# A non-local block on one core: the small tiles are allocated first and the large ones start on multiples of 2 KB

## What is computed

```
q = theta_w @ x + theta_b          # 256 x 1024 positions
p = maxpool2(x)                    # 1024 channels x 256 positions
k = phi_w @ p + phi_b              # 256 x 256
v = g_w @ p + g_b                  # 256 x 256
a = softmax(q.T @ k * 256**-0.5)   # 1024 x 256
out = z_w @ (v @ a.T) + z_b + x    # 1024 x 1024
```

## The kernel before

| kind | function | stationary | moving | columns | matmuls in all |
|---|---|---|---|---|---|
| q | `project_q` | theta | x_split | 512 | 3072 |
| k | `project_k` | phi | xp | 256 | 1536 |
| v | `project_v` | xp | g | 256 | 1536 |
| s | `scores` | q | k | 256 | 1536 |
| a | `attend` | vt | pt | 512 | 768 |
| z | `project_out` | z | att | 256 | 5376 |

## Time and profile before

### The profile page before, as it was taken

The page is one execution under the profiler, slowest core; times in us unless marked ns, Lnnn a source line. Parts: engine busy times, 40 slices in busy tenths (PEclk is TensorE's granted clock), DMA queues, the critical chain, the costliest instruction groups (busy, mean ns, idle before and its releaser), DMA issues.

```text
span 2162.6 us, 40114 instructions
## 1 busy us (share of the span) xinstructions
PE 2082.1 (96%) x13824; PEld 1898.1 (88%) x13824; DVE 1566.2 (72%) x2617; ACT 1293.1 (60%) x2228; POOL 1377.9 (64%) x835
## 2 busy tenths in 40 slices
PE   6799999999999999999999999999999999999996
PEld 5699989998998899899989988998999899999996
DVE  6877767876777777678767777776787677787765
ACT  4565656665656655566646656565666566666553
POOL 4666667765667666667656676665676566776653
PEclk9899999999999999999999999999999999999998
DMA  6455566564666565575655664655656556656535
GB/s 224 132 200 187 178 203 213 175 207 158 200 218 198 173 201 174 192 233 176 196 163 189 214 216 156 202 179 185 233 175 196 167 185 214 221 177 203 186 102 175
DMA packets 213070, 409.54 MB, mean 189 GB/s; under 512 B 12688, under 2 KB 15760, under 8 KB 212880
## 3 DMA queue, kind: packets, MB, share of 16 engines
q1 hardware_dynamic: 212736, 406.90, 56.9%
q10 hardware_dynamic: 144, 0.01, 0.0%
HBM read 272.64 MB, written 134.22 MB: 188 GB/s over the span
## 4 chain that ended last, share of the span: by engine, by line
PE 94%; DVE 2%; issue 2%; DMA 1%; ACT 0%; POOL 0%; SPq 0%; DVEq 0%
PE bank L748 94%; DMA x<-x 1%; DVE pt_raw L597 1%; DVE z_lo L636 0%; DVE phi_lo L561 0%; DVE x_top L615 0%; DVE x_bot L615 0%; DVE pooled L569 0%; ACT probs L408 0%; DVE att_f L627 0%; POOL x_split_lo L494 0%; POOL pt_lo L504 0%; POOL att_f L507 0%; DVE q_lo L575 0%; POOL att_lo L512 0%
## 5 line engine op out<-in xcount | busy, mean ns | idle before, releaser
L494 POOL TENSOR_TENSOR x_split_lo<-x,x_split_hi 128x1024 fp32r<-128x1024 f32 x256 | 617.4, 2417 | 278.4 <-ACT x_split_hi L320 278.4
L748 PE MATMUL bank<-att_hi,z_hi 128*128 128x256 f32 x1792 | 497.4, 278 | 8.1 <-POOL att_lo L512 5.1
L748 PE MATMUL bank<-att_lo,z_hi 128*128 128x256 f32 x1792 | 496.7, 277 | 0.0
L748 PE MATMUL bank<-att_hi,z_lo 128*128 128x256 f32 x1792 | 496.6, 277 | 0.0
L597 DVE STREAM_TRANSPOSE pt_raw<-probs 32x256 f32<-32x256 f32 x1024 | 446.1, 436 | 17.5 <-ACT probs L408 0.9
L512 POOL TENSOR_TENSOR att_lo<-att_f,att_hi 128x512 fp32r<-128x512 f32 (+1 forms) x192 | 282.9, 1480 | 216.7 <-ACT att_hi L359 216.7
L748 PE MATMUL bank<-x_split_hi,theta_hi 128*128 128x512 f32 x1024 | 407.7, 398 | 12.2 <-POOL x_split_lo L494 10.0
L748 PE MATMUL bank<-x_split_lo,theta_hi 128*128 128x512 f32 x1024 | 404.6, 395 | 0.0
L748 PE MATMUL bank<-x_split_hi,theta_lo 128*128 128x512 f32 x1024 | 404.0, 395 | 0.0
L615 DVE TENSOR_TENSOR x_top<-bank,x_top 128x512 f32<-128x512 f32 x512 | 334.9, 688 | 86.6 <-PE bank L748 79.7
L320 ACT ACTIVATE x_split_hi<-x 128x1024 fp32r<-128x1024 f32 x256 | 270.8, 1058 | 162.3 <-PE bank L748 158.8
(11 more groups left out here) (64 smaller groups left out, 4139.0 us busy)
## 6 DMA issues: line engine op xcount, KB each, us to landing
x<-x SPq DMA_DIRECT2D x256, 512.0 KB, 4.0
x_top<-x SPq DMA_DIRECT2D x128, 512.0 KB, 7.0
x_bot<-x SPq DMA_DIRECT2D x128, 512.0 KB, 7.8
out<-x_top SPq DMA_DIRECT2D x128, 512.0 KB, 3.6
out<-x_bot SPq DMA_DIRECT2D x128, 512.0 KB, 4.7
x_top<-theta_wt SPq DMA_DIRECT2D x4, 256.0 KB, 6.1
x_bot<-phi_wt SPq DMA_DIRECT2D x4, 256.0 KB, 9.5
x_top<-g_wt SPq DMA_DIRECT2D x4, 256.0 KB, 8.7
```

Source lines behind the costliest of these rows:

```text
L494: nc.gpsimd.tensor_tensor(flat(lo), flat(x_chunk(s, c)), raw(flat(hi)), ALU.subtract).then_inc(x_ready, 1)
L748: last = nc.tensor.matmul(dst, stationary(a), moving(b), start=start and n == 0, stop=stop and n == len(PRODUCTS) - 1, skip_group_check=re ...
```

## The change

The small tiles (`bias`, `phi_bias`, `negmax`, `rowsum`, `rowinv`: 32 or 64 bytes each after rounding, 192 bytes together) are allocated ahead of the large ones, followed by an unused tile `line_pad` of 704 bytes. 1152 + 192 + 704 = 2048, so `theta_hi` starts at byte 2048, and as all tiles up to `pt_lo` have sizes that are multiples of 2048 bytes, each starts on such a multiple. `att_f` loses its eighth block and moves behind `att`: `att_hi` starts at 206848 (101 x 2048), `att_lo` 7168 bytes behind it, on a multiple of 1024, and `att_f` at 221184 (108 x 2048). The fourth sum of the z weights goes to the first block of `probs` instead, and for that VectorE waits once for the transposes of the first step, which read `probs`. No instruction is added, taken away or moved otherwise; no shape changes.

```
+        bias = sb("bias", [P, NB], f32)
+        phi_bias = sb("phi_bias", [P, DT], f32)
+        negmax = sb("negmax", [P, NT], f32)
+        rowsum = sb("rowsum", [P, NT], f32)
+        rowinv = sb("rowinv", [P, NT], f32)
+        sb("line_pad", [P, 176], f32)
         theta = [sb(f"theta_{s}", [P, KT, D], f32r) for s in ("hi", "lo")]
...
         zw = [sb(f"z_{s}", [P, 7, TB * P], f32r) for s in ("hi", "lo")]
-        bias = sb("bias", [P, NB], f32)
-        phi_bias = sb("phi_bias", [P, DT], f32)
...
         probs = sb("probs", [P, NT, M], f32)
-        negmax = sb("negmax", [P, NT], f32)
-        rowsum = sb("rowsum", [P, NT], f32)
-        rowinv = sb("rowinv", [P, NT], f32)
         pt_raw = sb("pt_raw", [P, MT, H], f32)
         pt = [sb(f"pt_{s}", [P, MT, H], f32r) for s in ("hi", "lo")]
-        att_f = sb("att_f", [P, 8, HB], f32)
         att = [sb(f"att_{s}", [P, 7, HB], f32r) for s in ("hi", "lo")]
+        att_f = sb("att_f", [P, 7, HB], f32)
...
         def z_sums(i):
 
-            return flat(att_f)[:, i * WP:(i + 1) * WP]
+            return flat(att_f)[:, i * WP:(i + 1) * WP] if i < 3 else flat(probs)[:, :WP]
...
                 dve.wait_ge(z_sum, 3)
+                dve.wait_ge(pt_raw_done, P // Q)
                 nc.vector.tensor_tensor(z_sums(3), z_block(1), z_sums(2), ALU.subtract).then_inc(z_sum, 1)
```

## The result

The changed kernel is slower: 2198.8 us in the median of 4 runs (2196.65 to 2201.06), against 2168.32 us of the kernel before in 4 runs (2165.93 to 2170.78). The ratio is 1.0141, 95% interval [1.0123, 1.0158]; 2129 was forecast.

A forecast was written before the change was run, and what follows sets the result against it. TensorE's matmul count times start-to-start distance was taken as the bound; 25.6 us from s, k, v and 12.7 from q, a, about 38 after half clock, gave 2126.5 against the profiled 2164.45, so 2129 us for the median, range 2080 to 2172.

The forecast's parts named there:

- What bounds the kernel: Whole run: the number of TensorE matmuls times the distance between starts; TensorE 94% of the chain of waits.
- The gap ahead of s with k_lo as its releaser: Sign of a wrong forecast: idle time before the s matmuls, waiting for k_lo; 0.86 us of cover was expected to hold.
- The prices at half clock: TensorE at 1.2 GHz: exactly one column per cycle, 213.3 ns for s and 426 ns for a.
- a start off the 64-byte grid: 256-column matmuls: operands starting off multiples of 64 bytes go with 3.9 ns (v) or 6.2 to 6.6 ns (k, s) more.
- s 10.1, k 9.5 and v 6.0 us: Gains forecast for these three 256-column kinds from reaching z's 113.4 ns; 25.6 us together.
- z: both operands are on the grid already: 0: The z matmuls, 256 columns: starts already on multiples of 64 bytes, so no gain, 0 us.
- q and a: The 3840 matmuls of 512 columns: 3.3 ns less each from aligned starts, 12.7 us; bounds 0 and 77 us.
- It decides as soon as z goes over 113.4 by 0.8 ns: Sign for the slower rival about operands that start alike: z's distance rising above 113.4 ns by 0.8 ns.
- rival 3: 256-column matmuls: operands starting alike modulo 512 hinder each other; z and v lose 40 us together, 2208 us; chance 0.17.
- k is as slow as s at another remainder: Objection to the rival about operands starting alike: k equals s in pace though its start distance has another remainder modulo 512.
- Rival 2: Operand slices: crossings of 1 KB boundaries cost; q and a fall by 13.3 ns, 2091 us, down to 1999; chance 0.16.
- Rival 1: TensorE distances: operand starts don't matter, destination bank or product pattern does; time stays at 2168 us; chance 0.20.

The follow-up runs named there:

- Experiment 3: The changed kernel with every tile from theta on 32 bytes further, all distances between starts kept; 2195.62 us, ratio 1.0116 to the kernel before.
- Experiment 4: The kernel before with 320 bytes of padding ahead of att, so z's moving and stationary starts are alike; 2202.19 us, ratio 1.0140.
- experiment 2: The changed kernel with 192 bytes of padding ahead of att, so z's operands start 192 bytes apart again; 2178.16 us, ratio 1.0033 to before.
- experiment 10: The changed kernel with pads putting z's operands 192 bytes apart and those of q and a 96; 2171.09 us, ratio 1.0004 to before.
- the map: TensorE-only kernels, the computation left out, timing matmul blocks at varied operand starts; at 256 columns equal starts took 120.0 ns per matmul.
- experiment 8: TensorE-only kernel: 16-byte distance steps at two absolute starts, and blocks at distance 192 entered from 512-column blocks; distance 192 took 113.6 to 117.9 ns.
- experiment 5: TensorE-only kernel with all 64 pairs of stationary and moving remainders modulo 256; at 256 columns distance 192 took 113.3 ns twice, 117.8 six times.
- experiment 7: TensorE-only kernel of whole joined steps in real order under several placements; 37.81 us per step for the placement before, 38.17 for the changed one.
- experiment 12: The kernel before with pads around x_split and pt, so that q and a have operand distance 0; 2173.77 us, ratio 1.0014.
- experiment 11: The changed kernel with nine pads: q and a at distance 0, s, k, v and z at 192; 2142.42 us, ratio 0.9873 to before.

## Why the prediction was wrong

**What bounds the kernel** was right: TensorE's distances, no cover running out, nothing in the loop's steps eaten by another wait. The gap ahead of s with k_lo as its releaser, named as a sign of failure, did not come: s starts 0.79 us or more after k_lo ends. The prices at half clock, one column per cycle, hold: in both traces every kind has a median of 213 to 214 or of 427 ns there; only full-clock stretches differ.

**The step that failed first** is "a start off the 64-byte grid goes with 3.9 ns (v) or 6.2 to 6.6 ns (k, s) more". It read four kinds of one shape by one property, and four points fit more than one. Experiment 3 takes every large tile off that grid and nothing changes. What orders them is D: 192, 160, 96, 0 for z, v, k, s. The terms that hung on it, s 10.1, k 9.5 and v 6.0 us of gain, came out as 0.0, -0.5 and -4.1.

**"z: both operands are on the grid already: 0"** is the costliest step: +32 us. z was the fastest kind because its operands lay 192 bytes apart (and q before it 96), and the change took just that away. Experiment 4 shows it from the side of before, experiments 2 and 10 from the side of after.

**q and a:** the sign was right, the reason not. The gain is 4.5 ns instead of 3.3, 17.3 us instead of 12.7, and that the size came near is luck; at 512 columns D = 0 is the best distance, 226.7 ns, and the mean of 229.0 comes from the first six of each block, which still run at 226 to 236 (last section).

**"It decides as soon as z goes over 113.4 by 0.8 ns"**, of rival 3, is what held. Rival 3 (chance 0.17) had the mechanism: operands that start alike. It had z at 120.0 (measured 119.6) and v at 120.0 (measured 120.0), 40 us together; measured 36. It was wrong in two points: that q and a stay, and in the period, which is 256 bytes, not 512. Its objection, "k is as slow as s at another remainder", was no objection: the map has 120.0 both at D = 0 and at D = 96. So 2208 is 9 us above the result: less 17 for q and a, less 4 for z and v, plus most of what the turns add.

**Rival 2** (boundaries) falls with the maps: fixed distances of 512 to 2048 bytes are all 120.0, and q and a end at 229 and not at 220. **Rival 1** falls with experiment 4, where one pad costs 30 us.

**The rules weighed.** The rule of the Trainium skill, SBUF — State Buffer, Door 1, on 16-byte lines would have changed nothing, since all starts lie on multiples of 32; it does not reach this effect, as the traces differ by up to 6.7 ns at such starts. The other, TensorE: Matmul & The Clock Gate, Part 2, step 1, that TensorE has two independent read ports so that loading weights steals no bandwidth, was put against rival 3; here one pad that moves only the moving operand changes the pace of the pair by 5% (experiment 4), and moving both alike changes nothing (experiment 3), so the pace hangs on the two addresses together and is no free overlap at every placement. Where the two meet is not shown by any run.

**Not foreseen** was the part of the turns, some 15 us in the traces compared, of which experiment 3 repeats 8; its cause stays open.

## What to carry to other kernels

In a stream of weight loads and matmuls with 4-byte operands, look at the distance between the stationary and the moving start modulo 256 bytes and not only at each start's alignment, and weigh it by the number of matmuls of each kind: equal remainders, which rounding all tiles to a large power of two gives, were the worst case of the table at 256 columns (120.0 ns) and the best at 512 (226.7 ns). Neighbouring blocks influence each other, so measure whole steps in their order; a kernel with TensorE's stream alone gave the distances of the full kernel to about 1 ns, most of them to 0.2, and the placement found so took 1.3% off with unused tiles alone. And when a few kinds sort themselves by one property, ask which other properties sort them the same way before costing a change by it.

## What the runs showed of the hardware that was not expected

- At full clock a pair with 256 columns takes 113.3 to 120.0 ns, and one with 512 columns 226.7 to 236 ns, by D modulo 256 bytes, and the same at two absolute starts (experiment 8), for starts on multiples of 16 bytes; at half clock no such difference was seen: in the traces of before and after the median of every kind is 213 to 214 or 427 ns.
- Some distances have two paces at 256 columns: D = 192 has 113.3 or 117.8, D = 160 has 117.3 or 118.6, D = 208 had 117.8 and 119.2 in one map, and D = 32 ran at 117.8 in one map and 116.7 in another. For D = 192 it is picked on entering from the block before, within some ten matmuls, and then stays to the end of the block of 12 to 48 (experiments 5, 7, 8, 10, 12). Neither the D of the block before nor z's own start picks it alone (experiments 7, 8). Why is open.
- The first six matmuls behind a change of block can keep another pace: behind z at D = 0, q at D = 0 begins 233, 236, 228, 233, 231, 226 ns before it settles at 226.7. Behind z at 117.8 it is at 226.7 from the start (experiments 2 and 12), but behind z at 113.7 it begins 229, 233, 236, 224, 231, 236 ns and averages 231 (experiment 11). So what z gains at D = 192 is in part given back by q.
